# A fused decoder layer on one core: queues written out as single lists of steps, context loads moved ahead of wq, and ten matmuls of ones as TensorE's first work

## What is computed

```python
x = x + attn(layernorm(x))          # 8 heads of 128, 2 latent key/value heads of 32, causal softmax
x = x + xattn(layernorm(x), ctx)    # 16 heads of 16 over 77 context rows, then relu MLP 256-512-256
x = x + ffn(layernorm(x))           # two BitLinear layers 256-1024-256, gelu between
```

## Time and profile before

| | |
|---|---|
| median of three runs | 334.27 us |
| the profiled execution's own time | 336.98 us |
| its span, first to last instruction | 335.2 us |
| PE busy (matmul) | 304.6 us, 91% |
| DVE busy | 270.7 us, 81% |
| ACT busy | 187.8 us, 56% |
| POOL busy | 164.4 us, 49% |
| mean granted clock of TensorE | 0.979 |

### The profile page before, as it was taken

The page is one execution under the profiler, slowest core; times in us unless marked ns, Lnnn a source line. Parts: engine busy times, 40 slices in busy tenths (PEclk is TensorE's granted clock), DMA queues, the critical chain, the costliest instruction groups (busy, mean ns, idle before and its releaser), DMA issues. The chain is left out here.

```text
span 335.2 us, 8858 instructions
## 1 busy us (share of the span) xinstructions
PE 304.6 (91%) x3174; PEld 243.3 (73%) x3174; DVE 270.7 (81%) x488; ACT 187.8 (56%) x366; POOL 164.4 (49%) x315
## 2 busy tenths in 40 slices
PE   0799987999999999999999999999999989999524
PEld 0467766778878788878788888788878778868313
DVE  1024999799599999989997999799999979998562
ACT  1223612624534884388537963696278549679381
POOL 3425306708374558346636550745175617555751
PEclk9999999999999999999999999999999999999957
DMA  6998000000000000100000000000010010010000
GB/s 214 302 366 301 1 3 2 0 2 2 3 3 0 3 0 4 33 1 2 3 26 12 0 2 3 32 0 3 3 33 1 2 34 2 0 34 0 32 3 31
DMA packets 11732, 12.54 MB, mean 37 GB/s; under 512 B 1639, under 2 KB 10729, under 8 KB 11690
## 3 DMA queue, kind: packets, MB, share of 16 engines
q1 hardware_dynamic: 10970, 11.79, 11.0%
q10 hardware_dynamic: 720, 0.20, 0.3%
HBM read 9.89 MB, written 2.10 MB: 36 GB/s over the span
## 5 line engine op out<-in xcount | busy, mean ns | idle before, releaser
L632 ACT ACTIVATE c_p<-bank 77x512 f32<-77x512 f32 x64 | 36.8, 592 | 29.2 <-PE bank L1204 28.7
L1204 PE MATMUL bank<-ident,c_s 128*77 128x128 f32 x256 | 37.2, 276 | 0.2
L609 ACT ACTIVATE a_p<-bank 128x512 f32<-128x512 f32 x48 | 26.6, 599 | 14.3 <-PE bank L1137 14.3
L1227 PE MATMUL bank<-c_y,xw_s 128*128 128x128 f32 x256 | 31.4, 276 | 0.5 <-DVE c_y L879 0.5
L1227 PEld LDWEIGHTS bank<-c_y,xw_s 128*128 128x128 f32 x256 | 30.4, 192 | 1.4 <-issue 0.8
L1236 PE MATMUL bank<-xw_s,c_h 128*128 128x256 f32 x128 | 31.1, 386 | 0.0
L1204 PEld LDWEIGHTS bank<-ident,c_s 128*77 128x77 f32 x256 | 28.8, 148 | 2.8 <-issue 1.8
L411 POOL TENSOR_SCALAR c_ve<-c_mv 128x2 f32<-128x2 f32 x8 | 1.5, 192 | 56.9 <-DVE c_mv L779 56.9
L849 DVE TENSOR_REDUCE c_nm<-quad 128x16 f32<-128x1232 f32 x16 | 23.0, 1437 | 7.2 <-PE quad L1194 7.1
L683 ACT ACTIVATE f_hT<-bank 128x1024 bf16<-128x1024 f16 x16 | 16.3, 1020 | 20.6 <-PE bank L1265 20.6
L918 DVE SCALAR_TENSOR_TENSOR f_h<-bank,f_s,fb_s 128x512 f32<-128x512 f32 x32 | 22.2, 736 | 6.2 <-PE bank L1256 6.0
(11 more groups left out here) (136 smaller groups left out, 778.9 us busy)
## 6 DMA issues: line engine op xcount, KB each, us to landing
out<-f_o SPq DMA_DIRECT2D x16, 128.0 KB, 1.8
xres<-in_x SPq DMA_DIRECT2D x1, 1536.0 KB, 10.1
c_p<-in_wqT SPq DMA_DIRECT2D x2, 512.0 KB, 6.7
c_p<-in_wo SPq DMA_DIRECT2D x1, 1024.0 KB, 9.1
f_h<-in_fw1T SPq DMA_DIRECT2D x1, 1024.0 KB, 12.2
c_s<-in_fw2T SPq DMA_DIRECT2D x1, 1024.0 KB, 11.4
xw_s<-in_xw SPq DMA_DIRECT2D x2, 512.0 KB, 9.1
xres<-in_x SPq DMA_DIRECT2D x2, 256.0 KB, 5.1
```

Of the source, the lines that this page charges most:

```text
L609: nc.scalar.activation(dst, src, ACT.Exp, scale=SCALE_SA).then_inc(sa.sem["act"], 1)
L632: nc.scalar.activation(c_p[0:M, :, qt * P:(qt + 1) * P].rearrange("p (c j g) t -> p c j g t", c=KC, g=Q2)[:, :, j, :, :], bank("xs", f"tr{ ...
L1204: last = nc.tensor.transpose(dst[0:M, g * P:(g + 1) * P], c_s[:, qt, j, g, :], ident[:, :])
L1227: last = mm(bank("xm", f"w1{t}", i)[:, m * P:(m + 1) * P], xw1_s[:, c, m * P:(m + 1) * P], c_y[:, t, c, :], start=c == 0, stop=c == KC - 1)
```

## The change

Every engine's `iteration(k)` is replaced by a flat sequence of calls with the batch written out. The same order stands a second time as text in a table `ORDER`, from which `Steps` counts semaphore values and `Ring` takes the order in which banks are filled. The order is no longer periodic. No step is added or taken away, apart from the ten matmuls below. With it go the credits (the `sem_inc` loops), since a wait on a batch before the first is now a wait for 0.

```diff
+ORDER = dict(
+    pe="""
+        pro.v5.0 pro.v1.0 pro.v7.0 pro.wq0.0 sp.xT.0 pro.v0.0 pro.wq1.0 pro.wqk0.0 sp.k.0 pro.wqk1.0 pro.k3.0 sp.q.0
...
-    def after(self, eng, step, i):
-
-        return self.sem[eng], (max(i, -1) + 1) * len(self.names[eng]) + self.names[eng].index(step) + 1
+    def after(self, eng, step, i):
+
+        return self.sem[eng], self.count[eng, step, i] if i >= 0 else 0
+
+    def last(self, eng, steps, i):
+        return max((self.after(eng, step, i) for step in steps), key=lambda a: a[1])
...
+        def fills(table):
+            tensor = [s.split(".") for s in ORDER["pe"].split()]
+            return [(of, what, int(i), st[of].last(*table[of, what], int(i))) for of, what, i in tensor if (of, what) in table]
+
+        ring, quads = Ring(banks, fills(EMPTIED)), Ring([quad], fills(QUAD_EMPTIED))
```

The six context loads go ahead of `wkup` and `wqT`, `xv` gets a semaphore of its own, and `wkv` goes to ACT's queue of DMAs:

```diff
             sp.dma_start(xres[:, 0:TT, :], xin[:, 0:TT, :]).then_inc(ld_x0, 16)
-            sp.dma_start(wkup_s[:, :], wkupT).then_inc(ld_up, 16)
-            for c in range(KC):
-                sp.dma_start(wqT_s[:, 4 * c:4 * c + 4, :], ...
-            sp.dma_start(wkv_s[:, :, :], wkv.rearrange("(c p) d -> p c d", p=P)).then_inc(ld_kv, 16)
             sp.dma_start(ctxa[:, :], ctxT[0:P, :]).then_inc(ld_ctx, 16)
...
+            sp.dma_start(xv_b, xv[P:P + CK, :]).then_inc(ld_xv, 16)
+            sp.dma_start(wkup_s[:, :], wkupT).then_inc(ld_up, 16)
+            for c in range(KC):
+                sp.dma_start(wqT_s[:, 4 * c:4 * c + 4, :], ...
```

PE's first work, before any load is waited for (`WARM` is 10; `onesq` is a 128x128 tile that DVE sets to 1; `quad` is overwritten later):

```diff
+            pe.wait_ge(*pro.after("dve", "onesq", 0))
+            for n in range(WARM):
+                mm(quad[:, 0, 0:P], onesq[:, :], onesq[:, :], start=True, stop=True)
```

More of the change, by code:

```diff
@@ new lines, with __init__ @@
+QUAD_EMPTIED = {
+    ("sa", "suA"): ("dve", ("sbA0", "sbA1")),
+    ("sa", "suB"): ("dve", ("sbB0", "sbB1")),
+    ("xs", "su0"): ("dve", ("sb00", "sb01")),
+    ("xs", "su1"): ("dve", ("sb10", "sb11")),
+}
+class Steps:
+    def __init__(self, sems, of):
+        self.sem = sems
+        self.count = {}
+        for eng, order in ORDER.items():
+            mine = [s for s in order.split() if s.split(".")[0] == of]
+            for n, s in enumerate(mine):
+                _, step, i = s.split(".")
+                self.count[eng, step, int(i)] = n + 1
@@ L562, in _ @@
             pool.wait_ge(*pro.after("pool", "mhalf1", 0))
-            for k in range(FIRST, LAST):
-                iteration(k)
+            pro_ones()
+            sp_rstd(0)
+            sp_norm(0)
+            sp_rstd(1)
+            sp_norm(1)
+            sp_rstd(2)
+            sp_norm(2)
+            sp_rstd(3)
+            sp_norm(3)
+            xp_rstd(0)
+            xp_norm(0)
+            pro_t2()
+            pro_t1()
+            xp_b2(0)
+            xp_rstd(1)
+            xp_norm(1)
@@ L620, in xp_q @@
                 act.wait_ge(*xp.after("pe", "q", i))
-                act.wait_ge(*xs.after("pe", "su1", i - 2))
+                for qt in range(TT):
+                    act.wait_ge(*xs.after("pe", f"su{qt}", i - 2))
                 for c in range(KC):
@@ L764, in _ @@
             act.dma_start(identh[:, :], ident16_c[1].bitcast(F16)).then_inc(ld_cst, 16)
-            for g in st.values():
-                if g.credit("act"):
-                    nc.scalar.sem_inc(g.sem["act"], g.credit("act"))
-            for k in range(FIRST, LAST):
-                iteration(k)
+            f2_pre(0)
+            pro_wq(0)
+            f2_pre(1)
+            sp_xT(0)
+            pro_wq(1)
+            pro_wqk(0)
+            pro_wqk(1)
+            sp_k(0)
+            pro_k(3)
@@ L941, in f2_out @@
                     dve.wait_ge(out_sem[t], 16 * i)
+                else:
+                    for b in range(B):
+                        dve.wait_ge(*pro.after("pe", f"v{b}", 0))
                 nc.vector.scalar_tensor_tensor(f_o[:, t, :], bank("f2", f"l2{t}", i)[:, 0:D], f_hs[:, t:t + 1],
@@ L1039, in _ @@
+            f2_hq(7, 0)
+            f2_hq(7, 1)
+            f2_out(6, 1)
+            f2_out(6, 0)
+            f2_out(7, 0)
+            f2_out(7, 1)
         @block.tensor
```

1627 lines of the change are left out of this document (1252 added, 375 removed).

## The result

The changed kernel took **330.71 us** (median of 4 runs, 330.39 to 330.93) beside 334.23 of the kernel before (4 runs, 333.74 to 335.19), a ratio of 0.9891, 95% interval 0.9867 to 0.9914. The forecast was 324.9: right in sign, but 3.5 us were gained where 9.4 were forecast. A second comparison, with 23 runs of the kernel before, gave 329.02 beside 336.81, ratio **0.9799** (0.9764 to 0.9834), a gain of 7.8 us. Of the 4.3 us between the two gains, 2.6 come from the kernel before and 1.7 from the changed one; the first experiment looks at this. One more execution of the kernel before took 518.16 us at a mean granted clock of 0.57 and is left out everywhere.

The account below looks back on a forecast made before the run. PE was taken as the bound, saturated from 60 to 250 us. Gains of 3.0 (start), 0 (fill and middle), 3.4 (moved work) and 3.0 (shorter chain) sum to 9.4: 334.3 - 9.4 = 324.9 us, range 316 to 333.5.

Parts of the forecast that it names:

- The start, 3.0: First matmul and low clock: loss 12.7 us against 15.7, from loading the context earlier; a gain of 3.0 us.
- the clock term: At the start: 8.4 us of unbroken work at half speed, until 16.9 us, a loss of 4.2 us.
- the last of the sum: Whole kernel: the summed gain of 9.4 us subtracted from the median, 334.3, giving 324.9 us.
- The ten matmuls, 0: Ahead of the first v: matmuls on ones end some 4 us too early to help the clock; worth 0.
- The rival at 0.12: At the start: the ten matmuls hold the clock, the low-clock loss of 4.2 us goes, 320.7 us; chance 0.12.
- The fill and the middle, 0: PE's idle 3.6 us (40 to 60 us) and 2.2 us after stay; 0, bounds +5.8 and -3.6 us.
- the prediction's own sign of being wrong: In the middle, 60 to 250 us: PE busy over 99%; the prediction is wrong if the middle is not saturated.
- Work moved behind the last w2, 3.4: At the end: three hT and two l2 moved behind the last w2, which comes 3.4 us earlier.
- The shorter chain, 3.0: Behind the last w2: batch 7's first half goes five steps ahead, so the last half saves 3.0 us.
- The end was shorter: Rival at the end: added DVE and POOL steps leave it no shorter, 329.3 us; chance 0.17.
- On `quad`: Rival behind the fill: hand-overs of the single buffer quad stall PE at 28 places, up to 341.7 us; chance 0.10.
- That the change would do nothing: Rival for the whole kernel: gains are eaten in small waits, 333 to 335 us, no change; chance 0.08.

Follow-up runs that it names:

- the first experiment: The kernel before run again unchanged, 336.85 us (ratio 1.0009), and its order written as single lists without ones or credits, 336.13 us (ratio 1.0010).
- head_new: Against the kernel before: new loads, ten ones and the new order for TensorE's first 59 steps, then the old order on every engine; 331.63 us, ratio 0.9880.
- b28_end1: b_warm28 with five of TensorE's steps, and other engines' steps belonging to them, put behind the last w2; 338.94 us, ratio 1.0076 to the kernel before.
- a26_tog2: The changed kernel with 26 ones and both w2 of batch 7 together, DVE's and POOL's lists following; 333.55 us, ratio 0.9915 to the kernel before.
- b_again: The kernel before, unchanged, timed and profiled a second time; 336.85 us, ratio 1.0009.
- b_lists: The kernel before's order and loads written as single lists, without ones and credits; 336.13 us, ratio 1.0010.
- tail_new2: The kernel before's start, loads and middle, without ones, then the new order from xp.xT of batch 7 to the end; 340.18 us, ratio 1.0101.
- before: The first profiled execution of the unchanged kernel before, which the forecast was read from; 336.98 us.
- b_warm28: The kernel before's order and loads as single lists, with 28 ones as TensorE's first work; 332.47 us, ratio 0.9901 to the kernel before.

## Why the prediction was right and wrong

**The start, 3.0.** Its parts: first step 8.5 forecast, 8.23 found; `v` slow until 16.9 forecast, 18.06 found; loss 12.7 forecast, 8.2 + 4.9 = 13.1 found, against 15.7 before: 2.5. Right in these two profiles. What was not seen is that the clock term is no constant. "PE was busy ... 8.4 us of unbroken work; I give the new start the same" took one execution for a property of the kernel; in the eight profiles without splices at the end and without enough ones the loss was 1.7 to 5.9 us (5.2, 5.9, 2.7 and 3.2 in the old order, 4.9, 1.7, 5.0 and, in `head_new`, 4.7 in the new).

**The failed steps.** The larger is the last of the sum: "It was 2.7 us above the median of 334.27; I take the difference from the median". The terms were read from an execution of the upper level, and their sum was taken from a median of the lower one; 105 later runs have 71 at the upper. The second is a term: "3.4 us that the last `w2` comes earlier by, because PE is saturated ahead of it"; the work ahead of it fell by 1.8. Told by the two profiled executions, the 5.9 us by which the gain fell short (3.5 for 9.4) are:

| part | us |
|---|---|
| the sum taken from 334.23 and not from the 336.98 of the execution that was read | 2.75 |
| work moved behind the last `w2`: 1.8 for 3.4 | 1.6 |
| time outside the span: 2.6 for 1.8, taken as constant | 0.8 |
| the start: 2.5 for 3.0 | 0.5 |
| the chain behind the last `w2`: 2.7 for 3.0 | 0.3 |
| fill and middle: 0.1 for 0 | -0.1 |

Told by medians it is 2.6 for the kernel before (336.8 against 334.2), 1.7 for the changed kernel (its first four runs at 330.7, all above the later six at 329.0, whose profile loses 3.2 us less to the lower clock), and 1.6 because the gain was 7.8 and not 9.4. Both medians of the first comparison are unlike the later ones, each towards a smaller gain; whether that was luck or something in that comparison is not shown.

Two slips in the bounds changed nothing: if the slow stretch lasts 11.2 us in place of 8.4, the start loses 1.4 more and gains 1.6, not 1.1, and the upper end of the range is then 332.5 by its own terms, not 333.5.

**The ten matmuls, 0.** Right: 0 and 10 ones are not told apart. The reason holds too: 3.08 us of idle PE lie behind them and the granted clock is 0.50 from 7.82. The prediction set two statements of the Trainium skill (TensorE: Matmul & The Clock Gate, Part 1 and Why this matters for your kernels) against each other, that activity releases the throttle and that an idle stretch brings it back. The traces show both sides, with ten ones the second (the clock falls at 7.82, in the 3.08 us gap), and with 20 without a gap the first. But the prediction's own example from the end of the trace does not hold: there the clock had fallen at 317.82, ahead of the 5.19 us wait, which began at 319.60. The ones also lasted longer than forecast, 0.41 us each (4.07 for ten) and not 0.25, and ended 3.1 us ahead of the first `v`, not 4. The rival at 0.12, that the ones hold the clock, was a good idea with too few matmuls: twenty or 26 are worth 2.0 to 2.8 us (327.0 against 329.0 and, on one chip, 329.8).

**The fill and the middle, 0.** Right in sum by two errors that cancel. The fill gave back 2.5 (3.6 of idle to 1.1, without ACT's wait of 0.86), although I had argued that its waits were links of one chain; from 60 us to the last `w2` 2.4 more were idle, although PE was saturated there before. That the two are nearly equal is luck. Forecast and wrong: PE over 99% busy from 60 to 250 us; it was 187.60 of 190, 98.7%. That was the prediction's own sign of being wrong. In the new order PE waits there for DVE's division (`a_y`), its subtraction out of `quad` (`a_sA`) and its `h`, 1.3, 0.5 and 0.3 us; with the old order behind the new start (`head_new`) the only idle time there is just behind the join.

**Work moved behind the last w2, 3.4.** PE's work there, at the full clock, went from 7.5 to 11.2 us, 3.7: as forecast. Ahead of it the work fell by 1.8 only. What the other 1.9 us are is open: the same matmuls take 296.7 to 298.2 us in all, at the full clock, in seven profiles of the new order, and 295.4 to 296.3 in five of the old (profiles that lack a few records are at the lower end of each). And `b28_end1` shows that the step "because PE is saturated ahead of it" was no licence to move work: a saturated engine may be saturated with just the steps that cover its waits, and moved steps can hold up other engines' lists behind the last `w2`.

**The shorter chain, 3.0.** 2.7 found, 22.37 for 25.04. It varies: 22.4 in four profiles of the new order and 23.2 to 23.6 in three, 25.0 to 25.3 in four of the old. `a26_tog2` supports the head start as its cause, with the limit told there.

**The rivals.** The end was shorter, so that rival is out. On `quad` no wait of PE shows but that of the ones, so that one is out too. That the change would do nothing is out by 0.9799, and by 0.9891.

## What to carry to other kernels

Before a forecast takes a difference against a median, ask whether the executions of the kernel before lie at levels, and which one the profile and the median belong to; here the levels were 2.4 us apart, a quarter of the forecast, and the three runs of the median all fell on one while the profile fell on the other. Here matmuls of ones helped only when they ran on until the first real matmul; their number followed from the landing of the first load, and six too many cost nothing that showed, ten too few 2 us. Lists of several in-order engines are one object: a step moved on one alone cost up to 10 us, so an order is judged whole, and its cover is looked up before a step is taken away. A splice of two orders has to be checked for steps that pile up at the join, as the table loads did.

## What the chip showed that was not expected

The same matmuls in the same order have the clock raised after 5.3, 8.3 or 10.4 us of work at the start, in three executions of the old order (`b_again`, `b_lists`). A wait of 3 to 5 us ahead of the last `w2` cost more than itself: the granted clock fell in it and was 0.50 from 278.66 to 285.49 with the 4.7 us wait of `tail_new2`, and from 289.16 to 295.99 with the 3.4 us wait of `b28_end1`. Shorter waits came with a fall too, but not each time: in `b_again` the clock was 0.50 from 55.11 to 58.52 with waits of 1.22 and 0.57 us just ahead, and in `before` it stayed at 1.00 through the same waits (1.2 and 0.6); in `a26_tog2` it was 0.50 from 296.90 to 300.31, with waits of 1.21 and 1.61 us just ahead. In `tail_new2` the profiled execution took 336.84 and the other five 339.88 to 340.29; two of the five have the mean clock of the first, 0.985, so that column doesn't tell why. Between the span and the execution's own time lay 1.8 to 1.9 us in the kernel before, in `b_warm28` and in `head_new`, but 2.0 to 2.9 in the four and the six runs of the changed kernel; why is open.
